# A decoder layer on one core: the state-space stage takes its decay rows by DMA instead of by matmul, and attention computes one score product once instead of three times

## The reference, cut to what matters

```python
# state-space block, per sequence and head (b, h); the chunked form below sums to this
cum = cumsum(A * dt)                       # over the 128 tokens, A < 0, so cum falls
decay[s, l] = exp(cum[l] - cum[s])  if s <= l else 0
mix[s, l]   = decay[s, l] * (B[s] . C[l])  # B . C is shared by the heads of a group
y[l]        = sum_s mix[s, l] * dt[s] * x[s] + D * x[l]
hid         = y * silu(gate)
out        += norm_w * hid / rms(hid over a group of 4 heads) @ out_proj.T

# cross-attention
attn = softmax(q @ k.T)                    # every query sees all 2048 keys
attn = round(attn / s) * s                 # levels 0..255
out  = attn @ v
```

## Time and profile before

| | |
|---|---|
| median of 3 runs | 2147.5 us (2147.41 to 2147.55) |
| the profiled execution, its time | 2146.56 us |
| its span, first to last instruction | 2144.8 us |
| state-space stage, 16 units (one cycle) | 109.03 us, 8 times |
| attention, from 1212 to 1943 us | 731 us |
| busy over the span: PE, DVE, ACT, POOL | 84%, 77%, 78%, 27% |

### The profile page before, as it was taken

The page is one execution under the profiler, slowest core; times in us unless marked ns, Lnnn a source line. Parts: engine busy times, 40 slices in busy tenths (PEclk is TensorE's granted clock), DMA queues, the critical chain, the costliest instruction groups (busy, mean ns, idle before and its releaser), DMA issues. The chain is left out here.

```text
span 2144.8 us, 37991 instructions
## 1 busy us (share of the span) xinstructions
PE 1803.8 (84%) x12364; PEld 1273.8 (59%) x12514; DVE 1649.4 (77%) x2759; ACT 1665.4 (78%) x2987; POOL 580.7 (27%) x482
## 2 busy tenths in 40 slices
PE   6987999999999999999967677777777777774999
PEld 4775878787878787878746333333333333333887
DVE  5886686767686767676888699999999999994443
ACT  4666888888888888888826899999999999994211
POOL 2001555555555555555510000100000100003000
PEclk8998999999999999999989999999999999997999
DMA  4000000000000000000082499999999999995000
GB/s 139 16 6 30 0 30 0 29 0 29 0 29 0 29 0 29 0 26 4 0 182 39 78 182 183 185 184 184 180 185 185 183 183 180 186 186 122 11 11 20
DMA packets 566249, 173.94 MB, mean 81 GB/s; under 512 B 535168, under 2 KB 558592, under 8 KB 566144
## 3 DMA queue, kind: packets, MB, share of 16 engines
q1 hardware_dynamic: 566144, 172.57, 42.8%
HBM read 27.83 MB, written 2.10 MB: 14 GB/s over the span
## 5 line engine op out<-in xcount | busy, mean ns | idle before, releaser
L1223 ACT ACTIVATE levels<-s_ps,nb,qstep 128x512 int16<-128x512 f32 (+1 forms) x768 | 695.8, 915 | 32.7 <-DVE nb L1188 31.7
L1178 DVE TENSOR_REDUCE mx<-s_ps 128x1 f32<-128x512 f32 (+1 forms) x768 | 630.8, 862 | 26.4 <-PE s_ps L1128 26.4
L1128 PE MATMUL s_ps<-kT,qT 128*128 128x512 bf16 x1447 | 445.6, 386 | 200.1 <-ACT levels L1223 181.2
L603 DVE SCALAR_TENSOR_TENSOR xs<-x_ps,cw,xs 128x508 f32<-128x508 f32 (+2 forms) x393 | 291.2, 741 | 174.3 <-ACT xs L525 135.9
L1128 PEld LDWEIGHTS s_ps<-kT,qT 128*128 128x128 bf16 x1532 | 107.8, 97 | 434.8 <-ACT levels L1223 383.7
L659 POOL TENSOR_TENSOR hid<-y,sg 128x512 f32<-128x512 f32 x128 | 175.2, 1369 | 277.7 <-ACT sg L547 185.1
L494 PE MATMUL o_ps<-wo,hid 128*128 x1024 | 242.8, 380 | 4.9 <-DVE acc L590 4.9
L494 PEld LDWEIGHTS o_ps<-wo,hid 128*128 128x128 f32 x1024 | 192.7, 189 | 39.5 <-issue 9.8
L525 ACT ACTIVATE xs<-x_ps,cb,cw 128x512 f32<-128x512 f32 x131 | 101.9, 777 | 116.1 <-PE x_ps L446 116.1
L1246 POOL TENSOR_TENSOR sum_part<-sums 128x16 f32<-128x16 f32 x16 | 3.4, 211 | 689.5 <-ACT levels L1223 689.5
L1136 PEld LDWEIGHTS ao_ps<-vi,levels_T 128*128 128x128 f16 x4096 | 139.9, 96 | 66.9 <-DMA levels_T<-levels 7.6
(11 more groups left out here) (201 smaller groups left out, 3255.2 us busy)
## 6 DMA issues: line engine op xcount, KB each, us to landing
w_raw<-winT_dram SPq DMA_DIRECT2D x18, 512.0 KB, 4.5
wo_raw<-woutT_dram SPq DMA_DIRECT2D x9, 512.0 KB, 5.7
kT<-zeros SPq DMA_DIRECT2D x4, 1024.0 KB, 18.7
qT<-zeros SPq DMA_DIRECT2D x4, 1024.0 KB, 16.1
levels_T<-levels SPq DMA_TRANSPOSE x256, 4.6
acc<-xT_dram SPq DMA_DIRECT2D x4, 512.0 KB, 5.5
w_bc<-winT_dram SPq DMA_DIRECT2D x16, 128.0 KB, 2.4
acc<-x_dram SPq DMA_DIRECT2D x1, 2048.0 KB, 11.1
```

Of the source, the lines that this page charges most:

```text
L603: dve.scalar_tensor_tensor(to, x_ps[:, :, 0:SEQ - s], cw[:, head, TAPS - 1 - s], to, ALU.mult, ALU.add).then_inc(chain if s < TAPS - 1 els ...
L1128: return pe.matmul(s_ps[:, BANKS[h % 2][chunk], :], qT[:, qt, h, :], kT[:, h, at:at + GT], start=True, stop=True)
L1178: dve.tensor_reduce(mx[:, u, at:at + 1], src, AX.XY if what == "cd" else AX.X, ALU.max).then_inc(max_done, 1)
L1223: act.activation(levels[:, s, at:at + banks * GT].rearrange("p (c k) -> p c k", c=banks), s_ps[:, bank:bank + banks, :], ACT.Exp, bias=nb[ ...
```

## The change

In `front`, the three bf16 parts, the one-hot matrix and the wide bf16 mask are gone. The running sums are transposed in fp32 by four transpositions instead of sixteen, and four DMAs store them to a tensor in device memory (`rows`, one row of 2048 tokens for each head).

In `state_space`, SP loads for each unit the 512 sums of its head and token group, spread over the 128 partitions, into a ring of four buffers (`cum_row`). DVE then makes the exponent itself: `exponent(n)` is four instructions of 128x128, one for each sequence, `min(row + ncum, mask)`, at the end of its slot, for the unit that ACT needs in the next. ACT takes the exponential in one instruction of 128x512, in place. The matmuls into `d_ps` are gone; the bank that this frees makes `x_ps` double, so the projection of unit `m+3` waits for the convolution of `m+1` instead of that of `m+2`. The loops are written out, without registers; the weights of a ninth group, which nobody reads, are no longer prepared; two clears of PSUM are gone.

In `attention` the score of chunk b is issued once.

```diff
 # front, vector: the sums
-                    dve.tensor_copy(parts[:, :, 0, :], cum_ps).then_inc(chain, 1)
-                    dve.wait_ge(chain, next(step))
-                    dve.tensor_tensor(rest[:, :, :], cum_ps, parts[:, :, 0, :], ALU.subtract).then_inc(chain, 1)
...
+                    dve.tensor_copy(cum[:, :, :], cum_ps).then_inc(parts_done, 1)
 # front, gpsimd
-            pool.tensor_copy(mask[:, :], maskf[:, :]).then_inc(extra, 1)
-            pool.tensor_copy(onehot[:, :, :], sel[:, :].unsqueeze(2).to_broadcast([PARTS * H, H, P])).then_inc(extra, 1)
 # state_space, sync
+            sp.wait_ge(mem["rows_stored"], 16 * BG)
+            for n in range(UNITS):
+                r, h, g, tg, head = place(n)
+                if n >= RING:
+                    sp.wait_ge(d_ready, n - RING + 1)
+                sp.dma_start(row[:, n % RING, :, :].rearrange("p b l -> p (b l)"),
+                             mem["rows"][head:head + 1, tg * GT:(tg + 1) * GT].partition_broadcast(P)
+                             ).then_inc(row_loaded[n % RING], 16)
+                if n % (TG * HG) == TG * HG // 2 and g + 1 < G:
+                    load(g + 1)
 # state_space, tensor
-                    pe.matmul(d_ps[:, :, :], onehot[:, bass.ds(head_of(r, h), 1), :],
-                              cumT[:, bass.ds(r % TG * GT, GT)], start=True, stop=False)
-                    pe.matmul(d_ps[:, :, :], identb[:, :], mask[:, :], start=False, stop=True).then_inc(d_ready, 1)
...
+                    if n >= 2:
+                        pe.wait_ge(conv_done, n - 2 + 1)
+                    project(x_ps[:, n % 2, :, :], 0, n, x_ready)
 # state_space, scalar
-                    for b in range(BG):
-                        ex = act.activation(decay[:, h % 2, b, :], d_ps[:, b, :], ACT.Exp,
-                                            bias=ncum[:, bass.ds(r % TG * BG + b, 1), bass.ds(head_of(r, h), 1)])
-                    ex.then_inc(decay_ready, 1)
+                    act.activation(decay[:, n % 2, :, :], decay[:, n % 2, :, :], ACT.Exp).then_inc(decay_ready, 1)
 # state_space, vector
+            def exponent(n):
+
+                r, h, g, tg, head = place(n)
+                dve.wait_ge(row_loaded[n % RING], (n // RING + 1) * 16)
+                if n > 1:
+                    dve.wait_ge(mix_ready, n - 1)
+                for b in range(BG):
+                    ins = dve.scalar_tensor_tensor(decay[:, n % 2, b, :], row[:, n % RING, b, :],
+                                                   ncum[:, tg * BG + b, head:head + 1], mask[:, :], ALU.add, ALU.min)
+                ins.then_inc(d_ready, 1)
...
+                n = m + 3
+                if 0 < n < UNITS:
+                    exponent(n)
 # attention, tensor
                     pe.wait_ge(b_exp, n + 1)
-                    for _ in range(2):
-                        score(n + 2, "b")
                     score(n + 2, "b").then_inc(b_ready, 1)
```

More of the change, by code:

```diff
@@ L198, in _ @@
                     pe.wait_ge(parts_done, 1)
[L199 to L202, removed]
+                    for q in range(TG):
+                        tr = pe.transpose(ct_ps[:, q, :], cum[:, q * BG:(q + 1) * BG, :].rearrange("p b h -> p (b h)"),
+                                          mem["ident"][:, :])
                     tr.then_inc(ct_done, 1)
@@ L447, in project @@
                                        start=(k == 0 and s == 0), stop=(k == KE - 1 and s == 2))
                 mm.then_inc(ready, 1)
[L450 to L462, removed]
-                    pe.matmul(d_ps[:, :, :], onehot[:, bass.ds(head_of(r, h), 1), :],
-                              cumT[:, bass.ds(r % TG * GT, GT)], start=True, stop=False)
-                    pe.matmul(d_ps[:, :, :], identb[:, :], mask[:, :], start=False, stop=True).then_inc(d_ready, 1)
-                    if primed or n > 0:
+            for m in range(-LEAD, UNITS):
+                n = m + 3
+                if n < UNITS:
+                    if n >= 2:
+                        pe.wait_ge(conv_done, n - 2 + 1)
+                    project(x_ps[:, n % 2, :, :], 0, n, x_ready)
+                n = m + 2
+                if 0 <= n < UNITS:
+                    r, h, g, tg, head = place(n)
+                    if n:
@@ L501, in slot @@
                                            start=(b == 0), stop=(b == BG - 1), skip_group_check=True)
-                    mm.then_inc(out_unit, 1)
-            for hh in range(HG - LEAD, HG):
-                slot(-1, hh, False)
-            with pe.Fori(0, ROUNDS) as it:
-                for hh in range(HG):
-                    slot(it, hh, True)
+                    mm.then_inc(out_done, 1)
         @block.scalar
@@ new lines, in _ @@
+            dve.memset(ones[:, :], 1.0).then_inc(consts, 1)
+            dve.memset(half[:, :], -0.5).then_inc(consts, 1)
+            dve.wait_ge(nw_loaded, 16)
+            exponent(0)
+            for h in range(HG):
+                rest_of_weights(0, h)
+            for m in range(-LEAD, UNITS):
+                if m >= 0 and m // HG % TG == TG - 1 and m // (HG * TG) + 1 < G:
+                    rest_of_weights(m // (HG * TG) + 1, m % HG)
+                if m > 0 and m % HG == 0:
+                    if m == HG:
+                        dve.wait_ge(acc_loaded, 16)
+                        dve.wait_ge(consts, 2)
+                    finish(m // HG - 1)
+                n = m + 3
+                if n < UNITS:
+                    r, h, g, tg, head = place(n)
+                    dve.wait_ge(tap_ready, n + 1)
+                    for s in range(1, TAPS):
+                        if s > 1:
+                            dve.wait_ge(conv_chain, n * 2 + (s - 1))
+                        to = xs[:, h, :, s:]
+                        dve.scalar_tensor_tensor(to, x_ps[:, n % 2, :, 0:SEQ - s], cw[:, head, TAPS - 1 - s:TAPS - s], to,
+                                                 ALU.mult, ALU.add).then_inc(conv_chain if s < TAPS - 1 else conv_done, 1)
+                n = m + 2
+                if 0 <= n < UNITS:
+                    r, h, g, tg, head = place(n)
+                    if n > 1:
```

289 lines of the change are left out of this document (120 added, 169 removed).

## The result

The changed kernel takes 2370.6 us (median of 4 runs, 2369.8 to 2371.5) against 2147.5 for the kernel before (4 runs, 2143.9 to 2147.6). The ratio is 1.105, with an interval from 1.103 to 1.106.

The account below looks back on a forecast made before the run. PE was taken to pace the state-space stage. DVE-POOL turns lengthen its cycle from 109.0 to 136.5 us, +216 in all; 2146.6 + 216 is 2362.6, and 0.9 for the median gives 2364 us, range 2262 to 2462.

Parts of the forecast that it names:

- DVE and POOL take turns: State-space stage: each instruction of one engine waits for a whole one of the other; forecast 2364 us, chance 0.45.
- turns half as strict: Rival, state-space stage: DVE wins some turns, pairs pass together, 3.39 us from `mix` instead of 4.65; 2270 us, chance 0.18.
- no turns at all: Rival, state-space stage: exponents slip between POOL's instructions without waiting, cycle about 103.5 us; 2103 us, chance 0.09.
- The weights did come free: State-space stage: weights come after the exponent, when POOL's three instructions are over, saving contention; 0.95 us a slot.
- Which slot is free of contention: State-space stage: POOL has nothing to run in a round's last slot, so three slots of four are contended.
- A contended slot: State-space slot where the exponents meet POOL's instructions: 2.43 + 1.25 + 4.65 = 8.33 us.
- The piece from `mix` to the next tap: Part of a contended state-space slot, holding the exponents and their waits for POOL: 4.65 us, without POOL 1.45.
- the piece from the first tap to `xdt`: DVE's work in a state-space slot from first tap to `xdt`, taken from the kernel before: 2.43 us.
- the uncontended slot: State-space slot, one of four, whose exponents do not wait for POOL: 4.29 + 0.84 = 5.13 us.
- The upper bound of 0.29: State-space stage: time of each exponent instruction if nothing overlaps, 0.29 us against the 0.21 taken.
- The step that failed: Attention: issuing chunk b's score once brings no gain; clock stays 1.0 and the unit 2.86 us.
- a rival at 0.23: Attention: PE's clock falls; 118 us more if low throughout, 40 if in parts, giving 2404 us; chance 0.23.

Follow-up runs that it names:

- the control: The changed kernel with `x_ps` single again and the mask still in SBUF: 2375.7 us, ratio 1.107.

## Why the prediction was right, and where its sum was not

The time came out within 7 us (2364 for 2371) and inside the range. But it is a sum of two errors that nearly cancel: 47 us too many in the state-space stage, 53 too few in attention. That they cancel is luck; what was foreseen is that the state-space stage gets slower by its contention with POOL, and by roughly how much.

**The mechanism of the state-space stage was right.** "DVE and POOL take turns: each instruction of one waits for a whole instruction of the other" held for the new instructions: three long ones of four, in three slots of four, a mean of 0.89 us for 0.9. Taking POOL out of the way (mask in PSUM) removed every wait, the control removed none, and moving the exponent past two of POOL's three instructions removed 196 of 284. The rivals "turns half as strict" and "no turns at all" are ruled out for pieces of 128 columns; with 64 columns the turns are not one for one, as the run with eight pieces shows. The weights did come free, 0.94 us a slot for 0.95. Which slot is free of contention was right as well.

**Its sizes.** A contended slot is 8.07 us (462.19 to 470.26) for 8.33. The piece from `mix` to the next tap is 4.62 for 4.65. What was mis-sized is the piece from the first tap to `xdt`: I took 2.43 from the kernel before and it is 2.20 (462.19 to 464.39). Three taps now stand back to back in 2.29 us, where before they took 2.51, with the loop's register arithmetic between them; the section on the change says that this arithmetic goes, and the sum gives it no term. In the uncontended slot two errors cancel: 2.20 for 2.43, and 1.06 (458.27 to 459.33) instead of 0.84 for four exponents; the spacing is 0.26 us and not 0.21. The upper bound of 0.29 was nearer. `finish` takes 2.86 (459.33 to 462.19) for 3.05. So a cycle is 132.5 for 136.5: 12 x 0.26 and 4 x 0.19 and 4 x 0.02 make 4.0, which is 32 us in eight cycles. PE's load was taken too low as well, which costs nothing here: it is busy for 109.7 us of the cycle (83%) where 98 (72%) were forecast, and in a round that lies wholly at the upper level still for 26.0 of 32.2.

The other 15 us are the ends. The sum counted eight full cycles. By the distance from `var` to `var`, seven cycles cost 23.5 each, 164.5; but up to the first `var` the kernel loses 1.7 us, while it fills its pipeline, and in the last three rounds 3.8 (32.2, 32.2 and 22.3 against 26.1, 28.1 and 28.7), for the last round has no exponents left to make. Together that is 170.0, and the stretch shows 169.4.

**The step that failed** is the one on attention: "No gain", and "the granted clock should stay 1.0 and the unit 2.86". The first half is true, the second is not. The prediction had this as a rival at 0.23, priced at "256 x 0.46 is 118 us" if the clock were low throughout, and at a third of that for the likelier case of parts. It is low throughout, and costs 53. The placing was too optimistic and the price too high. The price came from doubling all of PE's time in a unit, 1.66 to 3.3. PE is busy for 640 us in 256 units, 2.50 each: a product goes from 0.39 to 0.61, a pair from 0.60 to 1.03, but the sixteen small products into `ao_ps` only from 0.55 to 0.62. Nor is PE the bound at 2.50 of 3.09. What lengthens the unit by 0.21 is the path from the products over DVE's maxima to the bias: ACT's waits for it are 0.27 us a unit (60.8 in 700 us, 3.09 each) instead of 0.11 (25.1 in 650 us, 2.87 each, with three products), and its own instructions take 12.4 us more over the stage, 0.05 a unit.

That the three products were surplus work is true for the result and false for the time. Without the two that go PE does not stay at the upper level in that stage, in either kernel, and with them it does; and they cost nothing while they are there, since ACT sets the unit.

**What was a neutral item and stayed one:** the row loads (one wait, 4.7 us for the 4 put down) and with it the front and the two clears (-1.6 in all; no run separates them), and the second `x_ps` bank. The stretch between the two big stages is 3.1 us longer. It goes with the clock: in the four of the ten traces where 21 to 22 us of the stretch lie at the lower level (the changed kernel is one of them) it takes 136.5 to 137.1 us, and in the other six, with 14 to 17 us at the lower level, 132.7 to 134.0. The run with eight pieces has both parts of the change and is one of the six. What decides how long the clock is low there stays open.

**What stays open.** Why the clock goes to the lower level with one product and comes back and goes again with two: the runs show that it does, and not by what rule. No run holds the clock with PE work elsewhere, and none shortens POOL's instructions.

## What to carry to other kernels

Before adding an elementwise instruction to DVE, look what POOL runs beside that place: with both tensors in SBUF it can wait for POOL's instruction, and four or more in a row here waited for all three that POOL had there (4.1 us for 1.1 us of work). The trace books the wait as busy time; the shortest, median and longest duration of a line give it away. An operand in PSUM avoided it, and so did the slots in which POOL had nothing to run (1.13 us); behind the taps the four still met one POOL instruction of three. Before removing matmuls that look redundant from a stage that another engine bounds, look at the granted clock of the stage: the work may be what holds it, as the two products were here, which cost nothing with the clock up and whose removal costs 53 us. And where a forecast comes out right, compare it stage by stage, for its total can be right by two errors.

## What the runs showed of the hardware beyond that

The clock also falls in the state-space stage of the changed kernel, to a mean of 0.95 in the cycle shown, and this costs nothing, since PE waits for DVE there. Two ordinary rounds, by windows, one at 1.00 and one at 0.91, are equally long:

```profile
358.97:391.15 32.18, 26.00 (x138) 20.91 (x137) 30.76 (x46) 20.03 (x25) 15.20 (x12) 1.00 0.11 34
459.33:491.50 32.17, 28.80 (x141) 23.56 (x141) 30.75 (x46) 20.14 (x25) 15.20 (x12) 0.91 0.26 82
```

In attention a partly low clock costs more than its share: with two products the mean clock is 0.88, so that it is low for about a quarter of the stage (0.12 of 0.50), and the stage has lost 23 of the 53 us, over four tenths. The exponent's own speed is the same with the mask in PSUM and in SBUF: the shortest take 335 and 336 ns for 128 columns. For 64 columns the shortest takes 268: half the columns save 68 ns of 336, so that most of such a short instruction does not depend on its columns.
